# Attention: pair sums of E added once more, so that one row-sum matmul serves four key steps

## The reference

```python
x = x + 0.5 * ffn(layernorm(x), fp4 weights)       # 512 -> 2 x 1408 -> 512, SiLU gate, RMS norm
x = x + attention(layernorm(x), Wq, Wk, Wv, Wo)    # 16 heads of 32, causal, 2048 tokens
x = x + 0.5 * ffn(layernorm(x), the same weights)
# attention: softmax(Q K^T / sqrt(32), causal) V, then Wo
```

## Time and profile before

| what | us |
|---|---|
| median of 3 runs | 2520.51 (2520.47 to 2521.26) |
| the profiled execution | 2520.36 |
| span of its instructions | 2518.6 |
| PE busy | 2447.1 (97%) |
| DVE busy | 1761.7 (70%) |
| POOL busy | 1540.1 (61%) |
| ACT busy | 1477.6 (59%) |

### The profile page before, as it was taken

The page is one execution under the profiler, slowest core; times in us unless marked ns, Lnnn a source line. Parts: engine busy times, 40 slices in busy tenths (PEclk is TensorE's granted clock), DMA queues, the critical chain, the costliest instruction groups (busy, mean ns, idle before and its releaser), DMA issues.

```text
span 2518.6 us, 40155 instructions
## 1 busy us (share of the span) xinstructions
PE 2447.1 (97%) x14559; PEld 1069.1 (42%) x14559; DVE 1761.7 (70%) x2956; ACT 1477.6 (59%) x2827; POOL 1540.1 (61%) x1596
## 2 busy tenths in 40 slices
PE   6999999999999999999999999999999999999998
PEld 3444444444443433333344433434334444444443
DVE  7966666667659595958576686868577766666665
ACT  7766666665225656566522356565674566666665
POOL 5577776674325667677332367676873566776775
PEclk9999999999999999999999999999999999999999
DMA  2022101121122111000320312020005101111101
GB/s 69 34 84 76 68 34 43 42 101 68 34 61 63 25 34 37 23 21 4 144 91 21 91 30 55 6 53 6 20 4 214 63 26 43 51 51 51 51 34 51
DMA packets 78118, 130.61 MB, mean 52 GB/s; under 512 B 19648, under 2 KB 24795, under 8 KB 77791
## 3 DMA queue, kind: packets, MB, share of 16 engines
q1 hardware_dynamic: 77918, 128.05, 16.5%
HBM read 68.23 MB, written 31.46 MB: 40 GB/s over the span
## 4 chain that ended last, share of the span: by engine, by line
PE 78%; DVE 9%; POOL 7%; ACT 2%; issue 2%; SPq 2%; DMA 1%; POOLq 0%; DVEq 0%; ACTq 0%
PE pp L97 59%; PE ps L97 17%; POOL sb L106 6%; DVE sb L118 3%; DVE sb L112 3%; ACT sb L103 2%; SPq L139 2%; PE ps L100 1%; DVE sb L106 1%; POOL sb L109 1%; DVE sb L109 1%; PE pp L100 1%; DMA sb<-sb 1%; DVE sb L115 0%; DVE sb L136 0%
## 5 line engine op out<-in xcount | busy, mean ns | idle before, releaser
L97 PE MATMUL pp<-sb,sb 128*128 128x512 f16 (+7 forms) x11230 | 2055.2, 420 | 20.4 <-DVE sb L112 9.6
L106 POOL TENSOR_TENSOR sb<-sb,sb 128x512 f32<-128x512 f32 (+6 forms) x1345 | 1486.8, 1132 | 947.3 <-ACT sb L103 321.7
L97 PEld LDWEIGHTS pp<-sb,sb 128*128 128x128 f16 (+3 forms) x11230 | 775.8, 101 | 1048.0 <-issue 232.7
L97 PE MATMUL ps<-sb,sb 128*128 128x512 f16 (+7 forms) x2786 | 720.3, 347 | 20.0 <-DVE sb L112 10.6
L103 ACT ACTIVATE sb<-pp 128x512 f32<-128x512 f32 (+7 forms) x1018 | 515.5, 548 | 285.1 <-PE pp L97 273.0
L118 DVE TENSOR_REDUCE sb<-pp 128x1 f32<-128x512 f32 (+2 forms) x720 | 453.6, 668 | 191.3 <-PE pp L97 188.9
L103 ACT ACTIVATE sb<-sb 128x512 f16<-128x512 f32 (+4 forms) x513 | 325.9, 649 | 353.2 <-DVE sb L112 293.2
L112 DVE SCALAR_TENSOR_TENSOR sb<-pp,sb,sb 128x512 f32<-128x512 f32 x447 | 324.6, 746 | 148.8 <-PE pp L97 133.0
L112 DVE SCALAR_TENSOR_TENSOR sb<-ps,sb,sb 128x512 f32<-128x512 f32 x437 | 318.3, 747 | 156.1 <-PE ps L97 128.4
L97 PEld LDWEIGHTS ps<-sb,sb 128*128 128x128 f16 (+3 forms) x2786 | 254.3, 98 | 340.8 <-DVE sb L118 36.5
L103 ACT ACTIVATE sb<-ps 128x512 f32<-128x512 f32 (+5 forms) x490 | 269.7, 557 | 151.2 <-PE ps L97 121.1
(11 more groups left out here) (29 smaller groups left out, 367.4 us busy)
## 6 DMA issues: line engine op xcount, KB each, us to landing
sb<-sb SPq DMA_DIRECT2D x144, 128.0 KB, 2.4
sb<-L_attn_X SPq DMA_DIRECT2D x64, 256.0 KB, 3.4
sb<-xa SPq DMA_DIRECT2D x64, 256.0 KB, 4.4
sb<-xc SPq DMA_DIRECT2D x64, 256.0 KB, 3.5
xa<-sb SPq DMA_DIRECT2D x32, 256.0 KB, 2.0
xc<-sb SPq DMA_DIRECT2D x32, 256.0 KB, 4.4
out<-sb SPq DMA_DIRECT2D x32, 256.0 KB, 2.0
sb<-sb SPq DMA_DIRECT2D x48, 96.0 KB, 2.1
```

What stands on the lines that cost most here:

```text
L97: return self.e.matmul(*a, **k) if self.e else self
L106: return self.e.tensor_tensor(*a, **k) if self.e else self
```

## The change

A second addition ("quad") joins the first. For each n with n % 4 == 3, `add_pairs` adds the pair sum in the slot of step n-1 to the pair sum in the slot of step n-3 (columns `offset(n-1)` to 512), on VectorE (two heads in one instruction, signal `dve_summed`) for the steps in `self.by_dve`, else on GpSimd (one head each, `pool_summed`). The planner chooses by its estimates, and puts all those of the late steps on VectorE. A "total" then comes once in four steps and always takes all 512 columns. The slot of step n-3 is held until the total; the slot of step n-1 until the second addition. Two more places in SBUF serve as slots: six from n = 16, seven from n = 48, eight from n = 88, six again from n = 120. Several prices of the planner are new, and ScalarE's scores may run further ahead when no max units are left (14 and not 7). In the first FFN, `decode` of chunk 2 comes before `weight` 2 and `vectors` and not after them.

```diff
@@ Ffn.order
                     if first and n == 0 and c == 0:
+                        yield "decode", 2, 99
                         yield "weight", 2
                         yield "vectors",
...
-                    if first and c == 0 and i == 0:
-                        yield "decode", 2, 99
@@ Att
-                  [QS0 + 98304, QS0 + 106496, C0, C0 + 8192]]
+                  [QS0 + 98304, QS0 + 106496, C0, C0 + 8192, C0 + 16384, C0 + 24576]]
@@ Att.order
-            return sum_end.get(k + 1)
+            return summed.get(k + 1) if k % 4 else sum_end.get(k + 3)
...
-            most = range(NE) if n < 16 else (0, 1, 2, 3, 6, 7) if n < 120 else range(6)
+            most = range(NE) if n < 16 else (0, 1, 2, 3, 6, 7, 8, 9)[:6 + (n >= 48) + (n >= 88)] if n < 120 else range(6)
...
-        line = [x for k in range(0, N, 2) for x in
-                [("total", k - 1) if x == "T" else ("weigh", k + int(x)) for x in '0T1'] if x[1] >= 0]
+        line = [x for k in range(0, N, 4) for x in
+                [("total", k - 1) if x == "T" else ("weigh", k + int(x)) for x in '01T23'] if x[1] >= 0]
+        summed, pending = {}, []
+
+        def second():
+            nonlocal dve, pool
+            n = pending.pop(0)
+            out.append(("quad", n))
+            ready, c = max(added[n], added[n - 2]), 512 - self.offset(n - 1)
+            on_dve, on_pool = max(dve, ready) + 4.16 * c + 64 + 301.700000, max(pool, ready) + 4 * (2.117 * c + 141)
+            if late or on_dve + 2352.000000 < on_pool:
+                self.by_dve[b].add(n)
+                dve = on_dve
+                summed[n] = dve + 145
+            else:
+                pool = on_pool
+                summed[n] = pool + 110
+
         while line:
+            while pending and max(added[pending[0]], added[pending[0] - 2]) <= max(pe, dve) + 291.000000:
+                second()
...
-            if ready and 4 * n + j < 4 * m + 8 + (7 if wide else 3):
+            if ready and 4 * n + j < 4 * m + 8 + (14 if wide else 3):
                 hunger = max(act - pe, 0)
-                cand.append((max(pe, clear[i], rowed[steps[n][0:2]]) + 0.050000 * hunger + (0 if first else 300.000000), "score", i))
+                cand.append((max(pe, clear[i], rowed[steps[n][0:2]]) + 0.011000 * hunger + (0 if first else 454.100000), "score", i))
...
-                    hunger = max(dve - pe, 0) + 6272.000000 * (lead - 0.096000)
-                    cand.append((max(pe, clear[i]) + 0.050000 * hunger, "max", i))
+                    hunger = max(dve - pe, 0) + 9178.000000 * (lead - 0.093590)
+                    cand.append((max(pe, clear[i]) + 0.011000 * hunger, "max", i))
...
@@ att_pe
-            off, last = t.offset(n - 1), kt == 4 * qt + 3
-            if kt == 1 and n > 1:
-                e.wait_ge(*t.inverted.at((b, *t.steps[n - 2][0:2], 0)))
-            e.wait_ge(*(t.late_added.at((b, n, 1)) if n in t.late[b] else t.e_added.at((b, n, 3))))
+            last = kt == 4 * qt + 3
+            if kt == 3 and n > 3:
+                e.wait_ge(*t.inverted.at((b, *t.steps[n - 4][0:2], 0)))
+            e.wait_ge(*(t.dve_summed.at((b, n, 1)) if n in t.by_dve[b] else t.pool_summed.at((b, n, 3))))
             for j in range(4):
-                k = e.matmul(RS[32 * j:32 * j + 32, off:512], p.ones[:, :], t.E[t.slots[n - 1][0]][:, j, off:512],
-                             start=kt == 1, stop=last)
+                k = e.matmul(RS[32 * j:32 * j + 32, :], p.ones[:, :], t.E[t.slots[n - 3][0]][:, j, :],
+                             start=kt == 3, stop=last)
@@ att_act
+            elif m % 4 == 0:
+                e.wait_ge(*t.sum_done.at((b, m + 3)))
             elif m % 2 == 0:
-                e.wait_ge(*t.sum_done.at((b, m + 1)))
+                e.wait_ge(*(t.dve_summed.at((b, m + 1, j // 2)) if m + 1 in t.by_dve[b] else t.pool_summed.at((b, m + 1, j))))
@@ new, called by att_dve and att_pool
+def add_pairs(e, p, b, n, made, many=2):
+
+    t, off = p.att, p.att.offset(n - 1)
+    for h in range(4 // many):
+        c, j = slice(many * h, many * h + many), many * h + many - 1
+        for k in (n - 2, n):
+            e.wait_ge(*(t.late_added.at((b, k, j // 2)) if k in t.late[b] else t.e_added.at((b, k, j))))
+        x = t.E[t.slots[n - 3][0]][:, c, off:512]
+        e.tensor_tensor(x, x, t.E[t.slots[n - 1][0]][:, c, off:512], ALU.add).then_inc(*made.up((b, n, h)))
```

More of the change, by code:

```diff
@@ L1345, in __init__ @@
         self.banks = [Banks() for _ in range(B)]
-        self.late = [set() for _ in range(B)]
+        self.late, self.by_dve = [set() for _ in range(B)], [set() for _ in range(B)]
         self.slots = {}
         self.late_added = p.sign("a_late_added")
+        self.dve_summed, self.pool_summed = p.sign("a_dve_summed"), p.sign("a_pool_summed")
         self.plan = [list(self.order(b)) for b in range(B)]
@@ L1432, in order @@
         total_units, total_scores = len(units), 4 * N
-        m, hold = 0, [None] * 8
+        m, hold = 0, [None] * 10
         def released(k):
@@ L1472, in order @@
             op, k = line[0]
-            can = k in added if op == "total" else 4 * n + j >= 4 * k + 4
+            can = k in summed if op == "total" else 4 * n + j >= 4 * k + 4
             if can:
-                ok = (max(added[k], inverted if steps[k][2] == 1 else 0.0) if op == "total" else
+                ok = (max(summed[k], inverted if steps[k][2] == 3 else 0.0) if op == "total" else
                       max(exped[k, 3], kept if steps[k][2] == 0 else 0.0))
-                begin = max(ok, pe + (100.000000 if mode == "row" else 0))
-                cand.append((begin + (300.000000 - 0.200000 * min(max(dve - pe, 0), 2000) - 0.000000 * min(max(act - pe, 0), 2000)
+                begin = max(ok, pe + (114.200000 if mode == "row" else 0))
+                cand.append((begin + (300.000000 - 0.200500 * min(max(dve - pe, 0), 2000) - -0.046310 * min(max(act - pe, 0), 2000)
                                       if mode == "row" else
-                                      0.000000 - 0.110000 * min(max(min(dve, act) - pe, 0), 2000)), "stay", 0))
+                                      3.538000 - 0.113600 * min(max(min(dve, act) - pe, 0), 2000)), "stay", 0))
+            if not cand:
+                second()
+                continue
             at, what, i = min(cand, key=lambda x: x[0])
@@ L1483, in order @@
                 if mode == "col":
-                    pe, mode = pe + 100.000000, "row"
+                    pe, mode = pe + 114.200000, "row"
                 at = max(pe, clear[i], rowed[steps[n][0:2]] if what == "score" else low_at if what == "rows" else 0.0)
@@ L1492, in order @@
                 if mode == "row":
-                    pe += 100.000000
+                    pe += 114.200000
                 mode = "col"
@@ L1572, in order @@
                               added[n] = pool + 110
+                  if n % 4 == 3:
+                      pending.append(n)
                   if steps[n][2] == 4 * steps[n][1] + 3:
@@ L1577, in order @@
                   n = step
-                  c = 512 - self.offset(n - 1)
-                  at = max(pe, added[n], inverted if steps[n][2] == 1 else 0.0)
-                  pe = at + 4 * c / 2.4 + 20
+                  at = max(pe, summed[n], inverted if steps[n][2] == 3 else 0.0)
+                  pe = at + 4 * 512 / 2.4 + 20
                   sum_end[n] = pe + 235
@@ L1584, in order @@
                       inverted = max(dve, sum_end[n]) + 745
-        for k in range(N - 2 + 1, N, 2):
-            self.sum_up(out, parts, k)
+        while pending:
+            second()
+        self.sum_up(out, parts, N - 1)
         yield from out
@@ L1797, in att_dve @@
                 add_steps(e, p, b, n, t.late_added)
+        elif what == "quad" and at[0] in t.by_dve[b]:
+            add_pairs(e, p, b, at[0], t.dve_summed)
         elif what == "invert":
@@ L1844, in att_pool @@
                 add_steps(e, p, b, n, t.e_added, 1)
+        elif what == "quad" and at[0] not in t.by_dve[b]:
+            add_pairs(e, p, b, at[0], t.pool_summed, 1)
         elif what == "level":
```

## The result

| | median us | runs |
|---|---|---|
| before | 2520.60 | 4 (2520.47 to 2521.26) |
| after | 2590.05 | 4 (2587.65 to 2594.34) |

The ratio is 1.0273, 95% interval 1.0262 to 1.0285: the change makes the kernel 69 us slower. I had forecast 2483. The profiled execution of after took 2591.45 us.

What follows compares the result with a forecast made beforehand. PE was taken to bound the attention. Both attentions' totals -54.8, visits -8, stalls +24 and ends +3, with the FFN's -1.8, gave -37.6 us on 2520.36, so 2483 was predicted, range 2460 to 2514.

Steps and rivals of the forecast that it cites:

- What bounds the kernel now: Attention: PE sets the time, busy 478.8 of 485 us; what is taken off it is gained unless another takes its place.
- Totals, -54.8: PE in both attentions: 72 full totals become 40 in each, 27.4 us less for an attention.
- Visits, -8: PE in both attentions: fewer visits to column work at 0.2 us each, 20 taken as falling away, 4 us for an attention.
- Second additions, and what they do to each other: Attention: 40 second additions, a full one 5.1 us on POOL or 2.36 on DVE; collisions charge DVE 1.5 us a quad.
- The balance, stalls of 24: Attention, 746 to 1196 us: PE 421, DVE and POOL 417 each; uneven load gives back 12 us for an attention.
- my sign of being wrong: Attention: the forecast counts as wrong if PE waits over 30 us in an attention, above all for L118.
- The end, +3: End of each attention: a second addition of 256 columns before the output projection adds 1.5 us for an attention.
- First FFN, -1.8: First FFN: the decode moved ahead fills VectorE's 1.84 us wait for ScalarE before weight 2, gaining 1.8 us.
- Slower: Rival, attention: no maximum is reduced during DVE's second additions, PE stands up to 2.6 us each; near 2530 to 2570; chance 0.10.
- Slots run out: Rival, first 16 steps of an attention: four waits of up to 5.1 us, 2493 to 2500 us; chance 0.06.
- The adding engines become the bound: Rival, attention: POOL and DVE need 430 to 447 us, stalls 20 to 28, time 2499 to 2515; chance 0.16.

Runs made afterwards that it cites:

- x1: The changed kernel without second additions on either engine, the reciprocal of the sums replaced by a constant: 2500.55 us, ratio 0.9914 to before.
- x13: x1 with VectorE's maxima reading half of their columns and every exp at scale 0: 2489.44 us, ratio 0.9872 to before.
- x12: x1 with the planner's prices of the kernel before: 2541.62 us, ratio 1.0079 to before.
- x3: The changed kernel with VectorE's second additions replaced by one-input maxima over the same elements, same place, waits and signals: 2515.86 us, ratio 0.9978 to before.
- x2: The changed kernel with all second additions outside the late steps on GpSimd: 2690.43 us, ratio 1.0667 to before.
- x8: The changed kernel with the planner told of collisions, by higher estimates for VectorE and GpSimd: 2601.26 us, ratio 1.0318 to before.
- x11: The changed kernel with the planner putting the combine ahead of second additions on VectorE: 2585.03 us, ratio 1.0249 to before.

## Why the prediction was wrong

*What bounds the kernel now:* right as to which engine, but "what is taken off PE is gained" held for a third: x1, with nobody in PE's place, gains 22 of the 61.6 us.

*Totals, -54.8:* the work is right (3200 passes for 3840), the gain was not to be had in full. x1 has it all, at no price for additions, and shows some 20 us beside the moved decode. In its first attention PE is idle for 8.6 us more than before, and some 3 us go to the lower clock. PE's weight loads wait longer for maxima, which hold the banks: before (first) and in x1:

```profile
PEld pp L97 <- DVE sb L118: 26.1, 49, 0.8
PEld ps L97 <- DVE sb L118: 15.9, 30, 1.3
```

```profile
PEld pp L97 <- DVE sb L118: 55.4, 107, 1.5
PEld ps L97 <- DVE sb L118: 18.9, 45, 1.4
```

Most of these 74 us (42 before) are hidden, as PE itself is idle for 14.8 us in all. The maxima are 11 us of what is missing (x13), and other prices move the time by 41 us (x12 against x1). The rest I cannot name.

*Visits, -8:* wrong in sign. Counted in the traces, the changes from row to column work are 153 in an attention of after and 143 before. At the 0.2 us that I took for a visit this is an estimated 2 us lost for each attention, and not 4 gained.

*Second additions, and what they do to each other:* their sizes were right. DVE took 21 of the 40. I charged 1.5 us of waiting to a quad; of DVE's 92.4 us, the eight late first additions take some 11 (in x3's groups they are 10.6), so 38 instructions took 81.4, 2.14 each, 0.96 above the 1.18 of an undisturbed one, or 1.9 for a quad. POOL's 417 us of the attention are within the 390 to 420 that I named; DVE's 440 are 30 above my 410, which was lower than my own sum (417 in the stretch to 1196, and 18 behind it). What I left out is the idle time ahead of them, 35.3 us, and that some wait out a whole run of GpSimd and not one instruction.

*The balance, stalls of 24:* **this is the step that failed.** I priced the collisions as capacity, and asked only whether three engines still fit into 421 us. Even that reading was too kind in one place: between 850 and 900 my own 36.6 + 8 + 4 = 48.6 us of POOL are over the 47, where I wrote that they fit. But capacity is not what ran out: DVE and POOL have slack in after, 84 and 107 of 524 us. With the same counts and the same order but one input, the kernel takes 2515.9. The collisions cost 74 us. The way they do is shown at the places read above (near 821, 950 and 1081 us): each engine follows a fixed order, a DVE instruction that stands for 2 to 6 us holds the maxima or the combine behind it, PE stands for what hangs on them, and the clock falls. For the first attention PE's idle time rises from 6 to 44 us, where I expected 18. That is my sign of being wrong (over 30 us), though most of its waits by name are for L106 of DVE (23.9 us) and not for L118 (8.3). And ten stretches at half clock, some 48 us together, take some 24 us of full speed, part of which PE would have waited anyway. PE's busy time, which I wanted 27 to 31 us lower, is the same. With the other terms as I had them (2459), the term of 24 measures 2590 - 2459 = 131 us: 89 for the second additions, and 42 that x1 lacks of its gain too, the wrong sign of the visits among them.

*The end, +3:* near. PE's last wait for the additions is 1.87 us, as one line of its timeline shows:

```profile
1269.19 1.06 PE L97 MATMUL pp<-sb,sb 128*32 128x512 f32 x8 [1.87 <-DVE sb L106]
```

*First FFN, -1.8:* right (1 to 5.5 measured, 1.56 in PE's timeline).

*The rivals.* "Slower" was the right mechanism and had 0.10: an addition on DVE during which no maximum is reduced, PE standing behind it. Its 2570 was 20 us short. I gave it 2.6 us at the most, and it is 4.9; I bounded both additions of a quad by 2.36 + 1.5 = 3.9 us, where 7.3 occur (at 820.83), and did not count DVE's idle wait ahead or the clock. My argument against it, that scores and weighs lie in between, does not hold where the combine, and with it the next query tile, is behind the addition. "Slots run out": not seen; PE's waits for ScalarE stay at 4 to 5 us. "The adding engines become the bound" did not come true as capacity anywhere: even in x2, with PE waiting for GpSimd, GpSimd is busy for 453 of 555 us.

The rule of the Trainium skill, "SBUF — State Buffer", section "SBUF: two separate sides", says under "Who interferes with whom" that a DVE instruction with at most one SBUF input, outside the 2-port perf modes, doesn't contend with GpSimd. x3 agrees: 1.21 us for each of the 38. The rule tells how two engines block; what that costs a kernel is in what stands behind them.

## What to carry to other kernels

Before moving additions of two SBUF operands to VectorE beside a busy GpSimd, replace them by a one-input instruction of the same size at the same place: the difference (74 us here) is what the collisions cost. With a fixed order on every engine a delay of a few microseconds on one of them became a stall of PE of nearly the same length here, and then a lower clock, so a budget of busy times is a lower bound and not a forecast; ask of each instruction that may be late what stands behind it. And when work is taken off the bound engine, run it with the replacement work left out first: that is the most the change can bring in this order (22 us here, for 62 worked out).

## What was not expected of the hardware

- A DVE addition beside back-to-back GpSimd instructions does not always wait for one of them. Of the 92 of 1024 elements in both attentions of after, 42 took 1.2 to 1.6 us and 44 took 2.0 to 2.3, but near 821, 950 and 1081 us one took over 6 us (near 821, to the end of GpSimd's run), and in other orders the longest took 8.3 (x8) and 9.5 us (x11). It comes back in the second attention, near 1537, 1666 and 1795 us. What decides between the two is open; it was not tried apart.
- The clock. In the kernel before PE keeps the full clock (mean 0.998) with 97% busy; after, the mean is 0.981. In its first attention there are ten stretches at half, and ahead of each PE had been idle, for 1.2 (twice in a row) to 5.0 us. With all additions on GpSimd the first attention has a mean of 0.91.
- Less work can be slower: x12 has 640 column passes fewer than the kernel before and no second addition, and takes some 20 us more. Its mean clock is 0.987, where the kernel before has 0.998.
